# Experts: one sorted set of 39 tiles in place of two sets of 19 and 27

## The reference

```python
def _L1_ffn_ref(x, W1, b1, Wg, bg, Wd, bd):     # x: 4096 rows of 128, HID = 512, E = 8
    H = gelu(x @ W1 + b1)                        # exact gelu
    probs = softmax(H @ Wg + bg)
    assign = argmax(probs)
    for e in range(8):
        y = H @ Wd[e] + bd[e]
        out = out + where(assign == e, probs[:, e] * y, 0)
    return out
x = x + _L1_ffn_ref(_layernorm(x), ...)
```

## Time and profile before

| what | value |
|---|---|
| time, median of 3 runs (lowest to highest) | 1478.36 us (1477.47 to 1480.76) |
| the profiled execution: its own time, and its span | 1475.8 us, 1474.0 us |
| PE busy | 1308.5 us (89%) |
| DVE busy | 1295.5 us (88%) |
| ACT busy | 1134.8 us (77%) |
| POOL busy | 813.3 us (55%) |

### The profile page before, as it was taken

How to read it: one execution, slowest core, us unless ns; L and a number is a source line. 1 busy time by engine, 2 the same in 40 slices (tenths; PEclk the granted TensorE clock), 3 DMA queues, 4 the chain that set the end, 5 groups by cost and what they waited for, 6 DMA issues and landing times. The chain is left out here.

```text
span 1474.0 us, 28531 instructions
## 1 busy us (share of the span) xinstructions
PE 1308.5 (89%) x7855; PEld 816.8 (55%) x7915; DVE 1295.5 (88%) x2296; ACT 1134.8 (77%) x1815; POOL 813.3 (55%) x1047
## 2 busy tenths in 40 slices
PE   5589999999987999999999986699999999989995
PEld 4434444444434888888888876344444444433564
DVE  5789999999988999999999986589999999966753
ACT  5466777777756999999999965587877787757873
POOL 4155554554545999999999975012233333216644
PEclk9799999999997999999999998799999999999998
DMA  6044545555518990000000002155555555304331
GB/s 255 1 143 171 200 175 196 191 185 193 199 57 266 335 326 3 0 0 0 0 0 0 0 0 115 58 204 196 193 183 195 199 194 181 110 1 127 96 92 31
DMA packets 65742, 186.76 MB, mean 127 GB/s; under 512 B 4463, under 2 KB 47479, under 8 KB 49178
## 3 DMA queue, kind: packets, MB, share of 16 engines
q1 hardware_dynamic: 62682, 179.74, 36.0%
q0 software_dynamic: 3008, 6.37, 1.2%
HBM read 145.51 MB, written 41.49 MB: 127 GB/s over the span
## 5 line engine op out<-in xcount | busy, mean ns | idle before, releaser
L942 PE MATMUL r_p_y<-w_ffn,r_z_t 128*128 128x128 f32 x1920 | 254.1, 275 | 26.5 <-ACT r_z_t L979 23.0
L942 PEld LDWEIGHTS r_p_y<-w_ffn,r_z_t 128*128 128x128 f32 x1920 | 254.1, 193 | 6.4
L1052 POOL TENSOR_TENSOR r_stat<-r_stat,minus_half 128x4 f32<-128x4 f32 x240 | 242.4, 1010 | 18.8
L567 POOL TENSOR_TENSOR b_lo<-b_prob,b_hi 128x1024 f16<-128x1024 f32 x32 | 79.9, 2498 | 257.9 <-ACT b_hi L538 257.9
L629 DVE SCALAR_TENSOR_TENSOR b_prob<-b_adj,b_prob 128x1024 f32<-128x1024 int32 x128 | 188.0, 1472 | 25.4 <-ACT b_prob L531 25.1
L629 DVE SCALAR_TENSOR_TENSOR a_prob<-a_adj,a_prob 128x1024 f32<-128x1024 int32 x128 | 187.0, 1463 | 17.8 <-ACT a_prob L531 17.8
L531 ACT ACTIVATE b_prob<-b_p_s,shift,g_unit 128x1024 f32<-128x1024 f32 x128 | 154.1, 1204 | 53.1 <-PE b_p_s L463 52.8
L531 ACT ACTIVATE a_prob<-a_p_s 128x1024 f32<-128x1024 f32 x128 | 131.1, 1024 | 72.6 <-PE a_p_s L463 72.6
L1011 DVE BATCH_NORM_STATS2 r_parts<-r_z 128x6 f32<-128x256 f32 x480 | 182.1, 421 | 1.3 <-ACT r_z L966 1.3
L567 POOL TENSOR_TENSOR a_lo<-a_prob,a_hi 128x1024 f16<-128x1024 f32 x32 | 82.6, 2581 | 173.4 <-ACT a_hi L538 173.4
L1004 DVE SCALAR_TENSOR_TENSOR r_h<-r_tanh,r_p_y 128x512 f32<-128x512 f32 x240 | 164.3, 684 | 4.5 <-ACT r_tanh L962 0.7
(11 more groups left out here) (295 smaller groups left out, 3055.0 us busy)
## 6 DMA issues: line engine op xcount, KB each, us to landing
a_adj<-in_adj_t SPq DMA_DIRECT2D x64, 1024.0 KB, 4.8
b_adj<-in_adj_t SPq DMA_DIRECT2D x64, 1024.0 KB, 4.8
sorted_rows<-blank SPq DMA_DIRECT2D x7, 4160.0 KB
x_got<-sorted_rows SPq DMA_DIRECT2D x46, 130.0 KB
sorted_rows<-blank SPq DMA_DIRECT2D x1, 4290.0 KB
x_rows<-in_x SPq DMA_DIRECT2D x4, 512.0 KB, 7.4
wd_raw<-in_wd SPq DMA_DIRECT2D x1, 2048.0 KB
late<-in_late SPq DMA_DIRECT2D x1, 756.0 KB
```

The source lines that it names most:

```text
L567: nc.gpsimd.tensor_tensor(lo[POOL_STEP][:], prob[POOL_STEP][:], hi[POOL_STEP][:], ALU.subtract).then_inc(s["lo_pool_ready"], 1)
L942: last = nc.tensor.matmul(out[:, D * t:D * t + D], z_t[g % R][:, P * t:P * t + P], k.w_ffn[:], start=False, stop=(t == TPC - 1), skip_grou ...
L1052: nc.gpsimd.tensor_tensor(stat[g][:, 1, :], stat[g][:, 0, :], k.minus_half[:], ALU.pow)\
```

## The change

There is one set of 8 chunks with 39 tiles (32 plus 7) in place of two of 19 and 27. The batches are nine of 4 tiles, one of 2 and one of 1 (11 in all), where there were 13. There is one table; it is made when the ranks of the last chunk are known. Nothing of the second pass stands between the chunks of the first any more: its first two transposes, its first `hidden`, and ScalarE's calls for it come behind the last `ranks`, and SyncE's first fetch waits for all 32 scatters.

```diff
-SET_CHUNKS = (3, 5)
+SET_CHUNKS = (CHUNKS,)
 SETS = len(SET_CHUNKS)
...
-SPANS = [4, 4, 4, 4, 3] + [4, 4, 4, 4, 4, 4, 2, 1]
-FIRST_B = 5
+SPANS = [4] * 9 + [2, 1]
...
     def sync(self, sp):
         for q in range(GROUPS):
-            part = 0 if q < FIRST_B else 1
-            if q in (0, FIRST_B):
-                sp.wait_ge(s["table"], part + 1)
-                sp.wait_ge(self.sent[part], 16 * TPC * SET_CHUNKS[part])
+            if q == 0:
+                sp.wait_ge(s["table"], 1)
+                sp.wait_ge(self.sent[0], 16 * TPC * CHUNKS)
...
     def tensor(self, pe):
         for c in range(CHUNKS):
             if c + 2 < CHUNKS:
                 turn_rows(c + 2)
-            elif c == CHUNKS - 1:
-                turn_rows(CHUNKS)
-                turn_rows(CHUNKS + 1)
-            hidden(c + 1)
+            if c + 1 < CHUNKS:
+                hidden(c + 1)
             if c > 0:
                 turn_logits(c - 1)
             for h in range(HC):
                 logits(c, h)
             if c > 0:
                 ranks(c - 1)
+        turn_logits(CHUNKS - 1)
+        ranks(CHUNKS - 1)
+        turn_rows(CHUNKS)
+        turn_rows(CHUNKS + 1)
+        hidden(CHUNKS)
+        pe.wait_ge(s["table"], 1)
         for q in range(GROUPS):
-            if q == 0:
-                layer(CHUNKS + 1, 0)
-                layer(CHUNKS + 1, 1)
-                turn_logits(CHUNKS - 1)
-                layer(CHUNKS + 1, 2)
-                layer(CHUNKS + 1, 3)
-                ranks(CHUNKS - 1)
-                pe.wait_ge(s["table"], 1)
-            elif q + 1 < GROUPS:
+            if q + 1 < GROUPS:
                 hidden(CHUNKS + q + 1)
-            if q == FIRST_B:
-                pe.wait_ge(s["table"], 2)
             if q + 2 < GROUPS:
                 turn_rows(CHUNKS + q + 2)
             products(q)
...
     def scalar(self, act, elu):
+        for c in range(CHUNKS - 3, CHUNKS):
+            exps(c)
         front(CHUNKS)
         front(CHUNKS + 1)
-        exps(CHUNKS - 3)
-        gelu(CHUNKS, 0)
-        gelu(CHUNKS, 1)
-        exps(CHUNKS - 2)
         for q in range(GROUPS):
             n = CHUNKS + q
-            if q > 0:
-                gelu(n, 0)
-                gelu(n, 1)
+            gelu(n, 0)
+            gelu(n, 1)
...
-            if q == 0:
-                exps(CHUNKS - 1)
...
     def vector(self, dve, leave, finish):
-            if c == CHUNKS - 1:
-                rows_low(CHUNKS)
-                rows_low(CHUNKS + 1)
...
-            if c == SET_CHUNKS[0] + 1:
-                table(0)
         copy_logits(CHUNKS - 1)
         places(CHUNKS - 2)
         weigh(CHUNKS - 2)
         choose(CHUNKS - 1)
+        places(CHUNKS - 1)
+        weigh(CHUNKS - 1)
+        table(0)
+        rows_low(CHUNKS)
+        rows_low(CHUNKS + 1)
         for q in range(GROUPS):
...
-            if q == 0:
-                places(CHUNKS - 1)
-                weigh(CHUNKS - 1)
-                table(SETS - 1)
             if q > 0:
                 send_back(q - 1)
```

More of the change, by code:

```diff
@@ L58 @@
 TAG, GATE = 2 * D, 2 * D + 1
-SET_CHUNKS = (3, 5)
+SET_CHUNKS = (CHUNKS,)
 SETS = len(SET_CHUNKS)
-SET_OF = [0] * SET_CHUNKS[0] + [1] * SET_CHUNKS[1]
-SET_ROW = (0, CHUNK * SET_CHUNKS[0])
+SET_OF = [0] * CHUNKS
+SET_ROW = (0,)
 SET_TILES = [TPC * n + E - 1 for n in SET_CHUNKS]
 MOST, TILES = TPC * max(SET_CHUNKS), max(SET_TILES)
-SPANS = [4, 4, 4, 4, 3] + [4, 4, 4, 4, 4, 4, 2, 1]
-FIRST_B = 5
+SPANS = [4] * 9 + [2, 1]
 STARTS = [sum(SPANS[:q]) for q in range(len(SPANS) + 1)]
@@ L1543, in products @@
                 pe.wait_ge(s["lt_copied"], CHUNKS)
-            if q == 1:
                 pe.wait_ge(s["taken"], CHUNKS + 1)
```

## The result

| | kernel before | changed kernel |
|---|---|---|
| median of 15 runs each, same chip (lowest to highest) | 1478.76 us (1474.32 to 1562.51) | 1480.7 us (1478.81 to 1484.91) |
| ratio of the times, 95% interval | | 1.002 [1.001, 1.0029] |
| span of the profiled execution | 1474.0 us | 1478.9 us |

The ratio puts the changed kernel about 2.9 us slower, between 1.5 and 4.3. The medians are 1.9 us apart; the ratio leaves out the one slow run of the kernel before (1562.51 us), and the means of the other runs are 2.9 us apart. The forecast was 1481.6 us with "slower" at 0.50 and "no measurable change" at 0.42, and the result lies almost on the line between these two.

The account below looks back on a forecast made before the run. TensorE was taken to bound the steady second pass, at 1.95 us a tile. Drain and refill delay batch 2's gelu by 17.7 us, less 14.45 for seven tiles: 3.2 longer, 1478.36 + 3.2 = 1481.6 us, range 1478.0 to 1485.2.

Parts of the forecast that it names:

- no measurable change: Rival for the whole kernel: the time stays within 0.2% (3 us) of before; chance 0.42.
- The tiles: Second pass: seven tiles fewer at about 1.95 us each save 14.45 us, bounds 13.6 to 14.98.
- The scatters: GpSimd, end of first pass: 20 more scatters, 1.27 us a step, 1.76 over three chunk borders; last starts at 1369.45.
- slack of 0.6: GpSimd's scatters at chunks 5 and 6: gates are ready some 0.6 us before the scatters need them.
- Landing and gathers: Between passes: scatter lands, eight gathers follow (7.63 to 8.22 us); batch 1's transposes start at T, 1383.3 (1382.8 to 1384.1).
- The refill: Start of second pass, from batch 1's transposes (T) to batch 2's gelu: T + 15.2 us, between 13.3 and 16.4.
- half-clock sum: Refill with TensorE starting at half clock: first gelu at T + 2.5, batch 0's products end at T + 15.5.
- upper end of 16.4: Refill with half-clock start and products of batch 0 at half clock too: batch 2's gelu at T + 16.4.
- the forecast's 13.3: Refill with TensorE's clock never low: batch 2's gelu at T + 13.3 us.
- A shorter scatter chain: Rival, GpSimd's scatters: 0.30 us less per step saves 5.7 us, ending at 1475.9; faster had 0.08 with the unknown.
- Late gates: Rival part, scatters at chunks 5 and 6: waiting for VectorE's gates adds about 1 us; no chance of its own.
- The rival of a cold refill: Refill at T + 16.4 alone: 4.4 us longer, 1482.8; chance 0.50 for slower, shared with the main sum.

Follow-up runs that it names:

- combined run: Changed kernel with the first eight gathers on two queues, the gelu table loaded early and idle matmuls around the first transposes: 1472.73 us, 0.9974 of before.
- the run of the three gaps: Changed kernel with idle matmuls in all three TensorE gaps around the refill (62, 16 and 6): 1479.44 us, 1.0017 of before.

## Why the prediction was right

**The tiles.** Forecast 14.45 us, bounds 13.6 to 14.98. The run with 46 tiles gives 14.2, with some 3.5 of uncertainty. Right.

**The scatters.** Right in the step of 1.27 and in the wait that goes; the last start was 1.07 us late. Of this 0.8 is the gate of chunk 5, where the forecast counted on a slack of 0.6 and named a late gate as what would move the end, and 0.2 is one scatter of 1.18 us. The same 0.97 or 0.98 us of idle time stands there in all variants read. The run with 28 scatters shows that the chain is on the path.

**Landing and gathers.** 2.47 and 0.83 us (forecast 2.43, 0.84); 7.63 for eight gathers, the lower bound; 2.05 to the eighth's landing, under the lower bound of 2.43. The forecast took the middle, so the gathers were mis-sized by 0.86 us, which offset the first gather's 1.10 of delay, and T came out 0.24 off: luck. The forecast's estimate of 2.3 us for such a transfer goes by what the Trainium skill (DMA: Bandwidth & Descriptors, Anatomy of one DMA — SWDGE (gpsimd) path) states for transfers that GpSimd issues, while SyncE issues the gathers. On a single queue the eighth gather took 2.05 here, with a second queue beside it 3.05.

**The refill.** T + 16.4 in place of 15.2: the step that was mis-sized, by 1.2 us. Up to the last high part of batch 0 the half-clock sum holds: products at + 15.5 less 6.4 of length and 0.8 ahead of them put it at T + 8.3, and it ended at T + 8.28. But the products began 1.87 us behind it, not 0.8: TensorE's four table reads, which the forecast put at nothing, ended only 0.3 us ahead of them. Then they took 5.41 us, between the 4.4 and 6.4 of the forecast, since the clock was low for part of their time, much as the 15.2 had assumed. So it is luck that the refill met the forecast's upper end of 16.4, which has products at half clock throughout: they began 1.05 us later than that line has them and took 1.0 less.

By the rule of the Trainium skill (TensorE: Matmul & The Clock Gate, HAM oscillation — how this bites in real kernels) that the forecast weighed, TensorE starts cold after a wait for transfers. The trace agrees for the first layer (0.50 over 1382 to 1386); the fall under the products came behind no wait for a transfer.

The way there was not all as argued in one more place. The sentence that ScalarE's table loads "now lie in an idle stretch" was wrong for the last of them: the gelu table is loaded behind the second front copy, 1.28 us on the path. At half clock it hides behind the first layer, so the changed kernel pays little for it; at full clock it is paid, and the forecast's 13.3 could not come from the clock alone. The combined run took both away and found 13.81; the 0.5 over 13.3 is the products' late start once more.

**The sum.** In the profiled executions batch 2's gelu moved by 19.1 us (1380.81 to 1399.94), forecast 17.7, and the end by 4.9, forecast 3.2. Over many runs the drain costs 17.1 and the tiles bring 14.2: 2.9 us slower, forecast 3.2. The 14.2 is the difference of two measured ratios, so this sum closes by itself; what is measured apart is the 17.1.

**The rivals.** A shorter scatter chain did not come: the 0.30 us stands in every step. Late gates came by 0.8. The rival of a cold refill has T + 16.4, 4.4 longer; the profiled execution has that length but was not cold all the way (clock 1.00 over 1390 to 1394), and the times lie below it. That the change is not to be told from none was nearly true.

## What to carry to other kernels

A seam between two passes is worth filling with padded work only as long as that work costs less than the drain: here seven padded tiles (14.2 us) were the cheaper way by 3 us, until the drain was shortened. A drain is a chain of single queues and cold engines, and its parts cover each other: table load and clock brought next to nothing each by itself in the times, and the second queue 4.0; all three brought 6.8 us together. Look also at what an engine reads for itself ahead of its work, as the table entries here: such reads show on no row of the engine's busy time. So try the parts one by one for the cause, and together for the gain.

## What the runs showed of the hardware

- Two queues that gather 130 KB tiles at once shorten the issue of eight by 4.3 us, but the last of them lands a microsecond later after its issue (3.05 against 2.05), so the gain was 3.3.
- A block of idle matmuls kept the clock at full speed for as long as it ran; one wait of 3.71 us for a transfer behind it, and the next 4 us were granted 0.50. In the combined run a wait of 1.74 us did no harm, and in the run of the three gaps one of 2.36. In the changed kernel the clock fell under the products at about 1395.5, though no wait since it had risen was longer than 1.36 us; why is not shown.
- The steady second pass has short dips of the granted clock (to 0.83 in a stretch of 10 us) that change their place from run to run; the one in the run of the three gaps held a batch up by some 3 us. Comparisons of two profiled executions carry that much noise, and only many runs settle 3 us.
- TensorE's four reads of table entries take some 2.6 us (1390.8 to 1393.4), and the first products follow 0.3 us behind the last one, 1.03 us behind the operand that they need.
